# Idle products of the identity between the row maxima of a two-layer transformer kernel

## The reference

```python
x = x + _layernorm(_L0_attn_ref(_layernorm(x), ...))   # 16 heads of 16, causal, rope
x = x + _layernorm(_L0_ffn_ref(_layernorm(x), ...))    # 8 experts, gated by the best 2
x = x + _layernorm(_L1_attn_ref(_layernorm(x), ...))   # 8 heads of 32, difference of two softmaxes
x = x + _layernorm(_L1_ffn_ref(_layernorm(x), ...))    # 64 experts, best 4, and 2 shared ones
```

```python
scores = jnp.einsum('bshd,bthd->bhst', q, k) / jnp.sqrt(HEAD_DIM)
scores = jnp.where(causal, scores, -jnp.inf)
probs = jax.nn.softmax(scores, axis=-1)
out = jnp.einsum('bhst,bthd->bshd', probs, v)
```

## Time and profile before

| | |
|---|---|
| runs before | 641.99, 652.14, 655.16 us, median 652.14 |
| profiled execution | 648.67 us, its span 646.9 us |
| mean granted clock | 0.811 |
| TensorE busy | 467.8 us (72%) |
| VectorE busy | 341.4 us (53%) |
| ScalarE busy | 234.8 us (36%) |

### The profile page before, as it was taken

How to read it: one execution, slowest core, us unless ns; L and a number is a source line. 1 busy time by engine, 2 the same in 40 slices (tenths; PEclk the granted TensorE clock), 3 DMA queues, 4 the chain that set the end, 5 groups by cost and what they waited for, 6 DMA issues and landing times.

```text
span 646.9 us, 8796 instructions
## 1 busy us (share of the span) xinstructions
PE 467.8 (72%) x2581; PEld 296.1 (46%) x2581; DVE 341.4 (53%) x1150; ACT 234.8 (36%) x473; POOL 179.5 (28%) x275
## 2 busy tenths in 40 slices
PE   1876759888786377779376868676669999999410
PEld 1433334433442245326245524443348888886300
DVE  5376684555434672523536136149726766663545
ACT  2222134332554164544235645342033443430215
POOL 5111012211232031321002322111165555504751
PEclk9897765555987598986868877878599999999775
DMA  6000010000000000000000300499035555533332
GB/s 201 16 2 1 8 42 0 2 1 1 0 1 2 0 2 0 17 2 0 1 0 1 99 0 2 152 390 302 7 91 158 163 161 163 163 98 123 105 103 68
DMA packets 29766, 42.82 MB, mean 66 GB/s; under 512 B 3616, under 2 KB 21024, under 8 KB 29728
## 3 DMA queue, kind: packets, MB, share of 16 engines
q1 hardware_dynamic: 25120, 29.74, 13.5%
q0 software_dynamic: 4608, 12.59, 7.4%
HBM read 31.83 MB, written 10.49 MB: 65 GB/s over the span
## 4 chain that ended last, share of the span: by engine, by line
PE 55%; DVE 21%; ACT 8%; issue 7%; POOL 5%; another core or an unknown queue 2%; DMA 2%; SPq 0%; DVEq 0%; ACTq 0%; POOLq 0%
PE PSUM L657 10%; PE PSUM L957 8%; PE PSUM L601 5%; PE PSUM L630 5%; PE PSUM L947 4%; PE PSUM L782 3%; PE PSUM L671 3%; DVE st L1236 2%; POOL QP L583 2%; PE PSUM L938 2%; PE PSUM L607 2%; DVE H L1246 2%; PE PSUM L594 2%; PE PSUM L818 1%
## 5 line engine op out<-in xcount | busy, mean ns | idle before, releaser
L1047 ACT ACTIVATE PR<-PSUM 128x1024 f32<-128x1024 f32 (+1 forms) x96 | 82.1, 880 | 83.1 <-PE PSUM L671 82.8
L536 POOL TENSOR_SCALAR_AFFINE_SELECT PR<-PR 128x256 f32<-128x256 f32 x128 | 52.9, 428 | 177.1 <-ACT PR L1047 176.4
L1317 DVE CUSTOM_DVE_ANT_0 XN<-PSUM,XN 128x128 f32<-128x128 f32 (+3 forms) x128 | 58.1, 489 | 48.4 <-PE PSUM L630 48.1
L573 POOL DMA_INDIRECT QP<-tokens,tok_of x64 | 60.8, 950 | 56.1 <-PE PSUM L938 24.1
L657 PE MATMUL PSUM<-PR,VA 128*32 128x256 f32 (+3 forms) x512 | 60.1, 566 | 12.1 <-DVE XT L1366 9.7
L957 PE MATMUL PSUM<-arena,QP 128*128 x256 | 66.0, 380 | 3.5 <-ACT QP L1196 3.5
L671 PE MATMUL PSUM<-QT,KTr 32*128 32x384 f32 (+7 forms) x256 | 53.0, 450 | 12.8 <-ACT PR L1047 10.2
L630 PE MATMUL PSUM<-KTr,QT 32*128 32x128 f32 (+3 forms) x128 | 43.4, 536 | 14.6 <-DVE mx L1317 14.2
L957 PEld LDWEIGHTS PSUM<-arena,QP 128*128 128x128 f32 x256 | 48.2, 190 | 10.6 <-issue 4.2
L404 POOL TENSOR_TENSOR QP<-QK,QP 128x128 f32<-128x128 f32 (+1 forms) x16 | 9.5, 591 | 148.2 <-ACT QP L397 80.2
L601 PE MATMUL PSUM<-wq_sb,XT 128*128 128x512 f32 x64 | 40.7, 771 | 6.6 <-DVE QK L1298 4.0
(11 more groups left out here) (238 smaller groups left out, 821.9 us busy)
## 6 DMA issues: line engine op xcount, KB each, us to landing
arena<-in_wgu SPq DMA_DIRECT2D x4, 2048.0 KB, 15.7
expert_outputs<-QP SPq DMA_DIRECT2D x64, 128.0 KB
arena<-in_wd SPq DMA_DIRECT2D x2, 2048.0 KB, 16.6
wq_sb<-in_wqkv SPq DMA_DIRECT2D x2, 768.0 KB, 5.4
X<-in_x SPq DMA_DIRECT2D x2, 512.0 KB, 4.6
QP<-in_wsgu SPq DMA_DIRECT2D x1, 1024.0 KB, 5.4
tokens<-XN SPq DMA_DIRECT2D x2, 512.0 KB, 12.8
QP<-tokens,tok_of POOLq DMA_INDIRECT x64
```

The costliest lines, as they stand in the source:

```text
L536: ins = pool.affine_select(diag, diag, [[0, 2], [1, P]], ALU.is_ge, 0.0, base=0, channel_multiplier=-1)
L573: pool.indirect_dma_start(out=XG[:, i % U, :], out_offset=None, in_=h_dram, in_offset=bass.IndirectOffsetOnAxis(ap=tok_of[:, i:i + 1], axis=0)
L1047: did(sc.activation(PR[:, n % PSLOTS, 2 * half:2 * half + 2, 0:WIDTH[chunk]], PSUM[:, 2 * half:2 * half + 2, 0:WIDTH[chunk]], ACT.Exp, sca ...
L1317: did(dv.tensor_tensor_reduce(MSK[m % 2][:, 0:nk], o[:, 0:nk], MASKQ[:, S - nk:S], op0=ALU.add, op1=ALU.max, scale=1.0, scalar=NEG, accum_ ...
```

## The change

It adds two kinds of products whose result nothing reads. Before each of the 64 maxima of batch 1, after the wait for its bank, TensorE multiplies the identity with itself into that bank: fp32, 128 rows by 128 columns of weights, 128 moving columns; the maximum's product then overwrites it. And `keep` multiplies the identity with up_sb (256 moving columns) into bank 4: 3 times behind each of the pairs 28, 29 and 30 of batch 0's maxima, 8 times behind pair 31, and 3 times behind the last turning, 20 in all. The first `keep` waits for the last projection's copy out of its bank (s_qkve) and for up_sb (s_w0).

```diff
+KEEP_AT = {28: 3, 29: 3, 30: 3, 31: 8}
...
+            def keep(n, o):
+                for _ in range(n):
+                    pe.matmul(o[:, 0:D], ident[:, :], up_sb[:, :], start=True, stop=True)
...
                     if kind == "max":
+                        pe.matmul(bank(6 + k % 2)[:, 0:P], ident[:, :], ident[:, :], start=True, stop=True)
                         maxima(1, n, bank(6 + k % 2))
...
                     for m in (2 * n, 2 * n + 1):
                         maxima(0, m, bank(m % 4))
+                    if n in KEEP_AT:
+                        if n == min(KEEP_AT):
+                            pe.wait_ge(s_qkve, NT)
+                            pe.wait_ge(s_w0, 64)
+                        keep(KEEP_AT[n], bank(4))
             pe.wait_ge(s_tev, 2 * NT)
             pe.wait_ge(s_qkve, NT)
+            keep(3, bank(4))
```

## The result

| | before | after |
|---|---|---|
| median | 651.52 us (4 runs, 641.99 to 655.16) | 686.59 us (4 runs, 685.10 to 692.98) |
| profiled execution | 648.67 us, span 646.9 us | 692.98 us, span 691.2 us |
| mean granted clock | 0.811 | 0.779 |

The ratio is 1.064, with a 95% interval of 1.047 to 1.081: the change makes the kernel 6.4% slower. The forecast was 640 us, in a range of 630 to 651.

What follows compares the result with a forecast made beforehand. It took TensorE's list at 1.2 GHz, tied to VectorE by bank round trips, as the bound. Opening +1.6, loop -9.1 and last weighing -1.4 summed to -8.9 from 648.67 us: 640 us, range 630 to 651.

Steps and rivals of the forecast that it cites:

- I take it that this holds 2.4 GHz through most of the stage: Batch 0's attention with batch 1's maxima: about three full products a step, beside weighing in half the steps, keep the clock high.
- rival (3): Loop: clock does not rise or falls back as the loop begins; products cost more, total 679 us; chance 0.08.
- 0.26 or 0.50 us a product: Price of each added identity product in front of a maximum, at 2.4 or 1.2 GHz.
- in the round trip in full and nothing hides it: Loop: each added product, between the bank's wait and the maximum, lengthens the TensorE-VectorE round trip by its whole time.
- the round-trip arithmetic of the loop: Bank round trips with the product, 1.54 us in tile 3 and 0.97 in tile 0; 32 make 40.2 us, +1.2 us.
- Weighing: -8.4: Loop: the 16.79 us of weighing take half the time at the high clock, saving 8.4 us.
- scores -1.5: Loop: scores run faster at the high clock, but most already fits into TensorE's waits; saves 1.5 us.
- turnings -1.0: Loop: four turnings speed up at the high clock, limited by ScalarE's unchanged copy; together save 1.0 us.
- the last weighing "-1.4": Behind the loop: the last weighing's 24 records, 2.79 us, take half the time, saving 1.4 us.
- End of the opening, "+1.6 us": Before the first scores: keep products behind pairs 28 to 31 and the last turning delay the scores by 1.6 us.
- VectorE's waits for L632 down by 8 to 10 us: Expected sign of success: VectorE waits 8 to 10 us less for the products of maxima.
- stages further on: Later stages, whose clock depends on where its falls happen to lie; no size forecast, chance 0.06.

Runs made afterwards that it cites:

- e3: Changed kernel with two identity products in front of each of batch 1's maxima in place of one; median 673.54 us, ratio 1.024.
- e9: Changed kernel with one bf16 product of 512 columns in place of each fp32 one, two per maximum in tile 3; median 652.32 us, ratio 1.002.
- e7: Changed kernel with no products before maxima, but two of 256 columns behind each step's maxima, 48 in all; median 651.12 us, ratio 1.002.
- e8: Changed kernel with the product before each maximum narrowed to 32 rows of the identity in place of 128; median 665.50 us, ratio 1.015.
- e11: Changed kernel with its own fp32 product moved ahead of the bank's wait, into weighing's free bank; median 696.68 us, ratio 1.072.
- e1: Changed kernel with only the 20 keep products, the 64 before batch 1's maxima taken out; median 650.27 us, ratio 0.993.
- e12: Changed kernel with bf16 products, two per maximum in tile 3, none in steps with the two longer weighings, 60 in all; median 682.27 us, ratio 1.042.
- e6: Changed kernel with 44 products of 256 columns behind maxima, fewer in weighing steps, none before maxima; four runs, 650.78 to 666.60 us, no verdict.
- e2: Changed kernel with only the 64 products before the maxima, no keep products; median 695.06 us, ratio 1.062.
- e4: Changed kernel with one bf16 product of 512 columns in place of the fp32 one before each maximum; median 650.02 us, ratio 1.003.
- e5: Changed kernel with the same 64 products bundled three in a row behind a step's maxima, in weighing's free bank; median 669.06 us, ratio 1.022.
- e10: Changed kernel with a bf16 product of 512 columns ahead of the bank's wait, in weighing's free bank; median 664.75 us, ratio 1.009.

## Why the prediction was wrong

**"I take it that this holds 2.4 GHz through most of the stage": this step failed.** The clock was 1.00 up to 99.2 us and 0.50 for the remaining 102 us of the loop. It is rival (3), at 0.08, in its second form: it "falls back as soon as the loop begins". The argument behind the step, that full products hold the clock and busy time as such does not, was supported: e3 and e9 held 1.00 through the whole loop, e7 for most of it. It was not isolated: no run has narrow products in the number in which full ones held the clock (e8 has one to a maximum, with which the full one failed too). What failed was the quantity. Three added products in a step were set beside stretches that had projections and turnings, and nothing was worked out about how much full work those had for each maximum. The prediction said itself that nothing of this kind, one full product to one narrow one, is in the trace; with that said, 0.08 for the rival was far too little.

The Trainium skill ("TensorE: Matmul & The Clock Gate", Part 1), which lets the clock follow how busy TensorE has been, does not agree with the trace after, as it did not with the one before: TensorE was busy for 101.08 of 102.40 us at 0.50 here, and for 62.90 of 64.89 us at 1.00 in e9. The slower rival, which the prediction put beside it, came near, but not by that rule: the clock did not run high already, it stayed low.

**"0.26 or 0.50 us a product": the wrong rows.** These were taken from full products one behind the other. Between narrow ones the same product costs 0.42 us at 2.4 and 0.72 at 1.2 GHz. The weight rows of tile 3 show that each one's weights begin to load only when it starts itself. In the stretch of the earlier trace rows they begin up to 0.11 us ahead (weights at 190.51 us for the product at 190.62). And e8 shows that the width matters, 0.45 against 0.72. Which of the two makes up the difference to 0.50 was not taken apart.

**"in the round trip in full and nothing hides it": right in its sum, wrong in its reason.** It is not hidden, but not because it stands behind the wait: e11 moved it ahead of the wait and nothing changed. It is not hidden because with it TensorE's list has no gap at all. For the same reason the round-trip arithmetic of the loop (1.54 and 0.97 us, mean 1.255) described a bound that was gone. Rival (3) counted half of each of the 64 products, since two banks share a round trip (16 us, and 3 for the scores); with TensorE as the bound each counts in full, 43.7 us by the trace for 42.1 found. That the rival's 679 us lies so near the 686.6 measured is luck: of its 30 us, the 11 for `keep` at the low clock did not come (the first scores stood 0.2 us later), and its 19 for the loop were 42.

**"Weighing: -8.4", "scores -1.5", "turnings -1.0", the last weighing "-1.4":** none came in the changed kernel, since all but the loop's first 6 us stood at 1.2 GHz; the last weighing took 2.58 us, against 2.79 before. In e9 the clock was there for all of them, and the stage gained 2.1 us in all where the prediction had 10.5 (9.1 and 1.4), with products dearer in sum, 80 x 0.32.

**End of the opening, "+1.6 us": nearly right.** The timeline of TensorE in the changed kernel, to be held against the earlier trace rows:

```profile
79.69 0.50 PE L632 MATMUL PSUM<-KTr,QT 32*128 32x512 f32 x2
80.11 1.56 PE L639 MATMUL PSUM<-up_sb,ident 128*128 128x256 f32 x6
...
87.05 0.50 PE L632 MATMUL PSUM<-KTr,QT 32*128 32x512 f32 x2
87.47 3.72 PE L639 MATMUL PSUM<-up_sb,ident 128*128 128x256 f32 x16
91.03 0.60 PE L645 MATMUL PSUM<-ident,QP 128*128 128x128 f32 x4
91.47 1.46 PE L639 MATMUL PSUM<-up_sb,ident 128*128 128x256 f32 x6
92.86 0.50 PE L679 MATMUL PSUM<-QT,KTr 32*128 32x512 f32 x2
```

From pair 28 to the first scores it takes 13.17 us where it took 10.98, +2.2, since pairs 30 and 31 took 0.43 and 0.42 us in front of their `keep` and the sum gave each about 0.25; the eight took 3.72 at 2.4 GHz (forecast 3.6), and the turnings 0.60 instead of 1.06. Pair 28 came 2.0 us earlier in this execution, with nothing changed ahead of it, so that the first scores stand at 92.86 and not at the 94.3 forecast. In the traces of e1 and e3 to e12, with the same opening, they stand anywhere from 93.27 to 98.41 us, so where they start decides nothing on a term of 1.6 us.

**"VectorE's waits for L632 down by 8 to 10 us":** they went up by 41. **"stages further on", 0.06:** two things there are as large as the effect that was forecast, the 8.0 us of batch 1's attention and the 10.5 us at the end.

**What stays open.** What VectorE waits for at the end of the kernel, 10.2 to 11.2 us, in nine of fourteen traces, and why it goes with the chip. Why the clock falls at different places in batch 1's attention. Why the kernel before took 650.51 to 661.84 us in 13 runs on one chip. Whether it is the rows of the array in use that hold the clock, or any added work in that number. What e6 would give.

## What to carry to other kernels

Work added to raise a clock has to be priced next to the neighbours that it will have and at both levels of the clock: here 0.42 and 0.72 us instead of 0.26 and 0.50, and the low level is the one that came. Ask first whether the engine's list still has gaps once the filler is in it; where it has none, the filler costs what it is long, and the best case (e9) was a draw. More filler can cost less than too little: e12 with 60 products was 4% slower than before and e9 with 80 of the same kind was not, and e3 with twice the change's products (673.54 us) lost less than one to a maximum on the same chip (e2, 695.06). Between these ends there are stages with part of the time at either level (e4, e5, e6, e7 and e10, at means of 0.70 to 0.89). And a stage and a total have to be compared like with like: e4 and e7 have a longer stage than the trace before and the same total as the runs before beside them, and the ends of two traces differed by 10 us from chip to chip.

## What the runs showed of the hardware

- A fully busy TensorE can stay at 1.2 GHz: 101.08 of 102.40 us busy at a granted 0.50, in a list that alternates products of 128 and of 32 rows. It went on running at 2.4 GHz with two fp32 products of 128 rows by 128 columns to each narrow one (e3), or one or two bf16 products of 512 columns (e9).
- A full fp32 product of 128 columns takes 0.26 us at 2.4 GHz behind its like and 0.42 in front of a narrow one; at 1.2 GHz it is 0.50 and 0.72. With 32 rows it is 0.45 at 1.2 GHz. A bf16 product of 512 columns takes 0.32 at 2.4 GHz, less than the fp32 one of 128.
- A product of 32 rows can run beside others on other rows, a full one does not: at 1.2 GHz maxima start 0.34 us apart with a narrow product each (e8), 1.23 with a full one, and the stage is 79.8 us instead of 109.0.
- The clock can stay low for long after one fall: in e12 it went down in tile 1, and the next 74.8 us ran at 0.50. It can also come back within a few microseconds, as in e6 (0.50 at 120 to 124 us, 1.00 at 136 to 140).
